# Attention values projected in the scan stage, key tiles turned one step later, layer 0's expert weights stored in the chip's tile layout

## The chip, the cores and the metric

The kernel runs on one core of a Trainium2 chip. The metric is the device time in microseconds of one execution of the whole program; lower is better. All arithmetic is in float32 except some masks in bfloat16.

## The reference

Two layers are applied to x (4 batches, 512 tokens, 512 features); `ctx` (4, 512, 256) is a second input.

```
x = x + mamba(ctx, layernorm(x))          # layer 0: selective scan, 512 channels x 16 states
x = x + moe0(layernorm(x))                # 32 experts, top 4, capacity 64, F = 352, and a shared expert
x = x + cross_attention(layernorm(x), ctx)  # layer 1: 16 heads of 32
x = x + moe1(layernorm(x))                # 32 experts in 8 groups, top 8, F = 256, and a shared expert
```

The cross attention, which the change touches most:

```
y_main, y_dca = ctx[:, :496], ctx[:, 496:]
q = ln(x @ Wq + bq)                     # per head, with weight and bias
k = ln(y_main @ Wk + bk);  v = y_main @ Wv + bv
out = softmax(q k^T * scale) v + softmax(q k_dca^T * scale) v_dca
out @ Wo + bo
```

The values `ctx @ Wv` depend on inputs only, not on anything that an earlier stage computes.

## The kernel before, in words

The program is a row of stages, each with one instruction stream per engine that is synchronised by semaphores; a stage ends with a barrier of all engines. The engines are TensorE (matrix products), VectorE, ScalarE and GpSimd; SyncE (SP) only issues DMAs.

**Scan stage** (`mamba_stage`, line 155). A loop of 64 iterations: 4 batches b, 16 states n each. In an iteration ScalarE makes `dA` (line 415), VectorE makes the input product and the scan (lines 505 and 511), GpSimd multiplies the states by C (line 285), and TensorE sums the products into `ps_y` (`total`, line 630). All are double buffered. Beside this, the same loop prepares batch b + 1: projection, convolution, the step sizes (`softplus` on TensorE at n = 12, its copies `summed` on ScalarE at n = 15), all through two PSUM banks `ps_w`. At n = 0 and 1 of the next batch TensorE turns the gated output of the last one back (`turned`). SP spreads rows of B and C over the partitions, four iterations ahead (`spread`). `ctxT`, the turned context of one batch, has one buffer.

**Layer 0's experts** (`expert_stage0`, line 1309). 16 tiles of 128 slots, two experts each. Weights of three tiles are held; SP loads those of tile t (`tile_weights`, line 1299) when the down projection of tile t - 3 is done. TensorE waits for all of a tile's loads before its gate product (line 1681). GpSimd adds each result to its tokens in DRAM by an indirect DMA (line 1437), one at a time: it waits for the landing of the one before. In DRAM the weights lie by expert as the reference has them, so a partition's row of a gate or up tile is 5632 contiguous bytes per expert, and one of a down tile 2048.

**Attention** (`attention_stage`, line 2051). The loop has 64 steps i: 4 batches b of n = 0 to 15, that is four groups g of four heads, four tiles j of 128 queries (for the scores that give the maxima) or keys (for the shifted scores). A step has, on TensorE, the shifted scores of i (line 2877), other work that the step number picks, and then the plain scores of i + 5 (line 2860), whose maxima VectorE takes (line 2616); ScalarE exponentiates the shifted scores (line 2378); GpSimd adds three of four probability tiles (lines 2241, 2248), and after four steps TensorE makes the sums (`SUM`, line 2893) and the weighted values (`PV`, line 2908; `DC` for the 16 DCA keys, line 2918). Step n = 0 has `PV` of the batch before.

The other work is named by a pair of letters: `K`, `Q`, `V` projections of the next batch's keys and queries and of this batch's values, `KT`, `QT` the normalised heads turned (line 2799), `XT` x turned, `M` the mixed queries, `AT` the turned maxima, `SD`, `PD` the DCA scores and probabilities, `WO` the output projection. All of these go through two PSUM banks, 6 and 7, in turn: the list `order` fixes the sequence, a name's bank is its number modulo 2, and `room(name)` makes TensorE wait until the name two places before it has been emptied by ScalarE or VectorE. The engines run their own instructions strictly in the order of the code. A head (K or Q tile) passes: TensorE projection, VectorE bias (`head_in`, line 2509), ScalarE square, VectorE variance (line 2519), GpSimd power and product (`head_norm`, lines 2224 and 2227), TensorE turn, ScalarE copy to `kT` or `rawq` (lines 2311, 2321). Heads have three buffers. In batch 0 the values and queries are made ahead of the loop. GpSimd also computes `rs`, the scale of the next batch's tokens (line 2218), which VectorE needs for `xn` (line 2499), and that is what `XT` turns.

In the steps 0 to 5 before the change, `order` reads for 1 <= b <= 2:

```
PV3 DC3 (b-1) SD0 K0 | SD1 K1 V0 V1 | M2 KT0 K2 V2 | V3 KT1 AT1 K3 XT0 PD0 SUM0 | PV0 DC0 KT2 Q0 | XT1 KT3 Q1
```

The exponentials of step i >= 4 wait until the `PV` that reads the same buffer is done, so those of n = 4 follow `PV0`.

## Time and profile before

| | us |
|---|---|
| median of 3 runs | 3114.5 (3114.5 to 3119.78) |
| profiled execution | 3106.26 |
| its span | 3104.5 |
| TensorE busy | 2687.9 (87%) |
| VectorE busy | 1493.2 (48%) |
| ScalarE busy | 773.7 (25%) |
| GpSimd busy | 1367.1 (44%) |

The span is the time from the first to the last record of one profiled execution. PE is TensorE, PEld its weight loads, DVE VectorE, ACT ScalarE, POOL GpSimd, SP the queue of SyncE. Busy shares are averages over stages with different limits; they say little on a change to one stage. L1681 is line 1681 of the kernel.

### The profile page before, as it was taken

The page shows a single profiled execution, that of the slowest core. Times are in us where ns is not written, and L with a number is a line of the kernel's source. Part 1 is how long each engine was busy: PE and PEld are TensorE (multiplying, and loading weights), DVE is VectorE, ACT ScalarE, POOL GpSimd, SP SyncE. Part 2 cuts the span into 40 slices and gives each one's busy share as a digit, 9 for nine tenths or more (in the row PEclk, how much of TensorE's full clock was granted, in tenths as well). Part 3 has the DMA queues.
Part 4 walks back from the last instruction along what each step waited for, and adds up shares of the span by engine and source line. Part 5 has one row for each costly group of instructions (what it writes and reads, how often), then busy time and mean ns, then how long its engine had stood idle before and what let it go on. Part 6 is the DMA issues. An engine that isn't in the chain of part 4 may idle for free. (4 is left out here: it accounts for less than half of the span.)

```text
span 3104.5 us, 33211 instructions
## 1 busy us (share of the span) xinstructions
PE 2687.9 (87%) x8933; PEld 1175.3 (38%) x8936; DVE 1493.2 (48%) x2766; ACT 773.7 (25%) x1190; POOL 1367.1 (44%) x960
## 2 busy tenths in 40 slices
PE   5888975799999887689999998981999999899995
PEld 2343431344444333233333334430444444444442
DVE  7999999332000232266666646310444444344442
ACT  4746653200000010133434332000121111111111
POOL 2777656143000131136646431465455555455555
PEclk8999999999999998889999999995999999999997
DMA  3334222310300599750474001555777776877664
GB/s 125 113 100 111 78 66 54 113 56 14 114 0 14 209 355 333 220 151 1 122 202 116 1 1 59 207 196 194 152 150 161 145 124 126 189 143 163 127 102 53
DMA packets 386408, 385.06 MB, mean 124 GB/s; under 512 B 72195, under 2 KB 311364, under 8 KB 386307
## 3 DMA queue, kind: packets, MB, share of 16 engines
q1 hardware_dynamic: 212434, 243.23, 25.0%
q0 software_dynamic: 68272, 97.19, 16.1%
q10 hardware_dynamic: 105600, 43.35, 6.6%
q8 instruction: 56, 0.92, 0.1%
q14 instruction: 46, 0.37, 0.0%
HBM read 236.15 MB, written 160.27 MB: 128 GB/s over the span
## 5 line engine op out<-in xcount | busy, mean ns | idle before, releaser
L1865 POOL DMA_INDIRECT out_x<-e_yo,e_dest x318 | 493.3, 1551 | 447.8 <-DMA out_x<-e_yo,e_dest 303.5
L2012 PE MATMUL e_psg<-e_wgu,e_xsT 128*128 x1272 | 578.3, 598 | 79.9 <-DVE e_xsT L1950 79.9
L285 POOL TENSOR_TENSOR hc<-hs,bcst 128x1024 f32<-128x1024 f32 x128 | 300.8, 2350 | 175.4 <-DVE ps_b L505 169.5
L2012 PEld LDWEIGHTS e_psg<-e_wgu,e_xsT 128*128 128x128 f32 x1272 | 233.1, 193 | 312.4 <-issue 312.4
L2028 PE MATMUL e_pso<-e_wd,e_hT 128*128 x636 | 306.2, 604 | 27.4 <-DVE e_hT L1955 26.7
L630 PE MATMUL ps_y<-hc,ident 128*128 128x512 f32 x512 | 242.5, 612 | 86.6 <-POOL hc L285 86.4
L511 DVE TENSOR_TENSOR_SCAN hs<-dA,ps_b 128x1024 f32<-128x1024 f32 x128 | 292.6, 2286 | 6.6 <-ACT dA L415 2.4
L1960 DVE TENSOR_TENSOR e_h<-e_psg,e_sg 128x256 f32<-128x256 f32 x159 | 67.3, 423 | 345.1 <-ACT e_sg L1886 335.3
L1233 PE MATMUL r_ps_t<-r_wd,r_h 128*128 128x512 f32 x480 | 209.6, 597 | 8.7 <-DVE r_h L982 5.1
L1886 ACT ACTIVATE e_sg<-e_psg 128x256 f32<-128x256 f32 x159 | 61.1, 384 | 543.9 <-PE e_psg L2012 538.5
L982 DVE TENSOR_TENSOR r_h<-r_ps_u,r_sg 128x512 f32<-128x512 f32 x60 | 41.4, 691 | 319.5 <-PE r_ps_u L1214 296.1
L415 ACT ACTIVATE dA<-dt,a_neg 128x511 f32<-128x511 f32 x256 | 165.4, 713 | 109.2 <-DVE hs L511 104.2
L2028 PEld LDWEIGHTS e_pso<-e_wd,e_hT 128*128 128x128 f32 x636 | 119.3, 191 | 188.5 <-issue 188.4
L2616 DVE TENSOR_REDUCE a_nm<-a_ps 128x2 f32<-128x992 f32 x128 | 146.1, 1185 | 88.9 <-PE a_ps L2860 88.5
L880 POOL DMA_INDIRECT slots_in<-r_xn,scat x128 | 126.6, 989 | 135.8 <-DMA slots_in<-r_xn,scat 60.3
L1893 ACT ACTIVATE e_yo<-e_pso,e_wrow 128x512 f32<-128x512 f32 x159 | 109.3, 687 | 288.4 <-PE e_pso L2028 217.4
L1950 DVE STREAM_TRANSPOSE e_xsT<-e_xs 128x512 f32<-128x512 f32 x159 | 174.6, 1098 | 12.8 <-DMA e_xs<-slots_in 7.3
L630 PEld LDWEIGHTS ps_y<-hc,ident 128*128 128x128 f32 x512 | 93.2, 192 | 230.7 <-POOL hc L285 135.7
L2378 ACT ACTIVATE a_pt<-a_ps 128x1024 f32<-128x1024 f32 (+1 forms) x128 | 126.2, 1022 | 184.0 <-PE a_ps L2877 123.3
L915 ACT ACTIVATE r_sg<-r_ps_g 128x512 f32<-128x512 f32 x60 | 35.8, 597 | 523.2 <-PE r_ps_g L1214 504.4
L505 DVE TENSOR_TENSOR ps_b<-du,bcst 128x1024 f32<-128x1024 f32 x128 | 159.3, 1244 | 8.3 <-DVE hs L511 0.5
L1214 PE MATMUL r_ps_g<-r_xnT,r_wgu 128*128 128x512 f32 x352 | 158.7, 593 | 0.0
(411 smaller groups left out, 3517.8 us busy)
## 6 DMA issues: line engine op xcount, KB each, us to landing
slots_in<-zeros SPq DMA_DIRECT2D x160, 256.0 KB, 2.3
e_xs<-slots_in ACTq DMA_DIRECT2D x160, 256.0 KB
bcst<-bc_rows SPq DMA_DIRECT2D x128, 256.0 KB, 4.3
e_wgu<-in_wg SPq DMA_DIRECT2D x32, 512.0 KB
e_wgu<-in_wu SPq DMA_DIRECT2D x32, 512.0 KB
e_wd<-in_wd SPq DMA_DIRECT2D x32, 512.0 KB
e_w<-in_wg SPq DMA_DIRECT2D x11, 1408.0 KB
e_w<-in_wu SPq DMA_DIRECT2D x11, 1408.0 KB
```

Of the source, the lines that this page charges most:

```text
L285: pool.tensor_tensor(hc[:, it % 2, half(h), :], hs[:, it % 2, half(h), :], bc(bcst[:, q, 1, :], 1, HB), ALU.mult).then_inc(sem["hc"], 1)
L415: i = act.activation(dA[:, it % 2, t, 1:], dt[:, b % 2, t, 1:], ACT.Exp, scale=a_neg[:, n, t:t + 1])
L505: dve.tensor_tensor(ps_b[:, :, :], du[:, b % 2, half(h), :], bc(bcst[:, q, 0, :], 1, HB), ALU.mult)\
L511: dve.tensor_tensor_scan(hs[:, it % 2, half(h), :].rearrange(flat), dA[:, it % 2, half(h), :].rearrange(flat), ps_b[:, :, :].rearrange(fla ...
L630: i = pe.matmul(ps_y[:, t, :], c["ident"][:, :], hc[:, it % 2, t, :], start=False, stop=False, skip_group_check=True)
L1214: i = pe.matmul(ps[:, f % 2, :], w[:, k, f * P:(f + 1) * P], xnT[:, b, k, :], start=k == 0, stop=k == KH - 1)
L1233: i = pe.matmul(ps_t[:, j % 2, :], h[:, f, j * P:(j + 1) * P], wd[:, f, :], start=f == 0, stop=f == FC - 1)
L1865: pool.indirect_dma_start(halves, bass.IndirectOffsetOnAxis(dest[:, q, a:a + 1], 0), yo[:, q, a * HC:(a + 1) * HC], None, bounds_check=2 * ...
L1950: dve.transpose(xsT[:, q % 2, :, :].rearrange("p k (s j) -> p k s j", j=DQ), xs[:, q // RING % 2, part, :].rearrange("p s (i k) -> p k s i ...
L2012: j = pe.matmul(ps_g[:, q % 2, :], xsT[:, q % 2, k, :], wgu[:, bass.ds(e % RING, 1), k, :], start=k == 0, stop=k == KH - 1)
L2028: j = pe.matmul(ps_o[:, q % 2, :], hT[:, q % 2, a, :], wd[:, bass.ds(e % RING, 1), a, :], start=a == 0, stop=a == NW - 1)
L2616: dve.tensor_reduce(nm[:, i % 8, 2 * z:2 * z + 2], ps[:, at:at + 2, 0:S2], AX_X, ALU.max, negate=True)\
```

## The change

1. *Scan stage.* It gets the weights `w_v` (loaded before the first row spreads), a buffer `vals`, and `values(b, ts)` on TensorE, ScalarE and SP: 16 projections of context tiles by `w_v`, copied and stored to a DRAM tensor `values`. Those of batches 1 to 3 are made at n = 13 and 14 of the batch before on TensorE and copied at n = 15 and n = 1 on ScalarE; those of batch 0 in the last batch, whose context is read again. The context loads move from n = 10 to n = 0, and `turned` waits for all four copies in the place of the step sizes.
2. *Attention.* The value projections, their copies and the weights `wv` go; SP reads the values of a batch from DRAM once `PV3` of the batch before has been computed. The zero fills that SP issues in batch 0 wait for nothing. `K3` moves ahead of the scores in n = 3; `KT1`, `KT2`, `KT3` move from n = 3, 4, 5 to n = 4, 5, 6; VectorE takes K3's bias at the start of n = 3 instead of after its maxima.
3. *Layer 0's weights.* The host stores, for a pair of experts, each partition's gate, up and most of the down weights in one row (`pair0`), and the last 96 rows of the down weights in `rest0`. `tile_weights` has three loads instead of six (four of them for down), and the down product reads its last chunk from its own view.

```diff
-    for w in ("wg", "wu"):
-        load(W[w].rearrange("p e k f -> p e (k f)"), I[w + "0"][2 * t:2 * t + 2, :, :].rearrange("e (p k) f -> p e (k f)", k=KH))
-    for z in range(2):
-        load(W["wd"][:, z, 0:2, :], I["wd0"][2 * t + z, 0:2 * P, :].rearrange("(c p) n -> p c n", p=P))
-        load(W["wd"][0:FR, z, 2, :], I["wd0"][2 * t + z, 2 * P:F0, :])
+    g = 4 * KH * F0
+    load(W["gate_up"], I["pair0"][t, :, 0:g])
+    load(W["down"], I["pair0"][t, :, g:])
+    load(W["down_rest"][0:FR, :], I["rest0"][t, :, :])
...
-        order += now(("SD", 1)) + new(("K", 1)) + late(("V", 0), ("V", 1))
-        order += now(("M", 2)) + new(("KT", 0), ("K", 2)) + late(("V", 2))
-        order += late(("V", 3)) + new(("KT", 1)) + now(("AT", 1)) + new(("K", 3), ("XT", 0)) + now(("PD", 0), ("SUM", 0))
-        order += now(("PV", 0), ("DC", 0)) + new(("KT", 2), ("Q", 0))
-        order += new(("XT", 1), ("KT", 3), ("Q", 1))
-        order += now(("M", 3)) + new(("XT", 2), ("Q", 2), ("QT", 0))
+        order += now(("SD", 1)) + new(("K", 1))
+        order += now(("M", 2)) + new(("KT", 0), ("K", 2))
+        order += new(("K", 3)) + now(("AT", 1)) + new(("XT", 0)) + now(("PD", 0), ("SUM", 0))
+        order += new(("KT", 1)) + now(("PV", 0), ("DC", 0)) + new(("Q", 0))
+        order += new(("XT", 1), ("KT", 2), ("Q", 1))
+        order += now(("M", 3)) + new(("XT", 2), ("KT", 3), ("Q", 2), ("QT", 0))
...
# SP, scan stage
+                sp.dma_start(w_v[:, :, :], I["wkv"][:, H:].rearrange("(k p) n -> p k n", p=P)).then_inc(sem["wvin"], 16)
                 for it in range(RING):
                     spread(it)
...
# ScalarE, scan stage
+                        if n == 1:
+                            values(b, (2, 3))
...
                         if n == 15:
                             summed(b + 1, range(TB))
+                            values(b + 1, (0, 1))
...
# TensorE, scan stage
+                def values(b, ts):
+                    turn = turn_of_values(b)
+                    pe.wait_ge(sem["wvin"], 16)
+                    pe.wait_ge(sem["ctxin"], 16 * (turn + 2))
+                    for t in ts:
+                        if t >= 2:
+                            pe.wait_ge(sem["vcopied"], TB * turn + t - 1)
+                        elif b > 0:
+                            pe.wait_ge(sem["dt"], TB * (b + 1))
+                        else:
+                            pe.wait_ge(sem["xadd"], TB * (B - 1))
+                        for k in range(KC):
+                            i = pe.matmul(ps_w[:, t % 2, :], ctxT[:, k, t * P:(t + 1) * P], w_v[:, k, :],
+                                          start=k == 0, stop=k == KC - 1)
+                        i.then_inc(sem["vmm"], 1)
...
# SP, attention
+                    if b == 0:
+                        context(2)
+                    else:
+                        landed(sp, ("PV", b - 1, NG - 1))
+                        values_in(b)
...
# ScalarE, attention
                     if more:
                         if n == 4:
                             squared(("K", b + 1, 3))
-                            keys(b + 1, 2)
+                            keys(b + 1, 1)
```

## Rows read from the trace of the kernel before

**Rows 1.** Stages: stretch, us; busy by engine; TensorE's clock, DMA share, GB/s.

```profile
0.00:552.00 552.00, 429.51 (x992) 178.57 (x993) 513.27 (x391) 296.20 (x440) 338.05 (x192) 0.95 0.32 91
...
1057.00:1283.00 226.00, 171.73 (x864) 77.58 (x864) 63.36 (x190) 24.44 (x42) 50.22 (x48) 0.89 0.94 305
...
1283.00:1882.00 599.00, 540.77 (x3168) 217.37 (x3168) 352.29 (x422) 213.90 (x274) 287.55 (x192) 0.96 0.35 95
```

**Rows 2.** Timeline (start, us, what, [idle before]) of SP and VectorE, scan start.

```profile
32.77 38.66 SPq L229 DMA_DIRECT2D bcst<-bc_rows  x12
...
48.44 1.23 DVE L505 TENSOR_TENSOR ps_b<-du,bcst 128x1024 f32<-128x1024 f32 x1
```

**Rows 3.** Timeline of TensorE, ScalarE, VectorE at the first batch boundary of the scan.

```profile
160.28 8.75 PE L630 MATMUL ps_y<-hc,ident 128*128 128x512 f32 x20
...
160.98 4.99 ACT L415 ACTIVATE dA<-dt,a_neg 128x511 f32<-128x511 f32 x8
...
168.29 2.29 DVE L511 TENSOR_TENSOR_SCAN hs<-dA,ps_b 128x1024 f32<-128x1024 f32 x1
```

**Rows 4.** Stretches, TensorE's timeline and the scatters' landing: layer 0's experts (third: attention).

```profile
1190.00:1194.00 4.00, 4.00 (x29) 2.10 (x26) 0.00 (x0) 0.46 (x1) 0.09 (x1) 1.00 1.02 391
...
1197.50:1200.00 2.50, 1.23 (x6) 0.14 (x2) 0.00 (x0) 0.69 (x1) 0.00 (x0) 1.00 1.08 264
...
1290.00:1297.00 7.00, 5.95 (x14) 3.46 (x15) 1.93 (x7) 1.20 (x2) 2.32 (x2) 0.56 1.05 393
...
1188.99 2.59 PE L1681 MATMUL e_psg<-r_wgu,e_xsT 128*64 128x352 f32 x16 [1.94 <-issue]
...
1203.35 4.57 PE L1681 MATMUL e_psg<-e_w,e_xsT 128*64 128x352 f32 x16 [4.62 <-issue]
...
x_after<-e_yo,e_dest POOLq DMA_INDIRECT x16, 8.6
```

**Rows 5.** Attention's costliest groups, and TensorE's timeline ahead of its loop.

```profile
L2767 PE MATMUL a_ps<-a_wv,a_ctxT 128*128 128x512 f32 x64 | 31.0, 608 | 7.7 <-DVE a_hd L2509 7.3 <-ACT a_v L2338 0.3
...
1302.94 1.96 PE L2767 MATMUL a_ps<-a_wv,a_ctxT 128*128 128x512 f32 x4 [0.87 <-DVE a_hd L2509]
...
1304.73 0.60 PE L2799 MATMUL a_ps<-ident,a_hd 128*128 128x128 f32 x4
...
1324.08 1.95 PE L2823 MATMUL a_ps<-a_rawq,a_mix 128*128 128x512 f32 x4 [0.96 <-ACT a_rawq L2321]
```

**Rows 6.** Timeline of GpSimd and TensorE in batch 1, n = 1 to 3.

```profile
1486.44 2.91 POOL L2224 TENSOR_TENSOR a_hr<-a_hv,minus_half 128x16 f32<-128x16 f32 x1 [18.34 <-DVE a_hv L2522]
...
1505.38 1.02 POOL L2218 TENSOR_TENSOR a_rs<-a_ve,minus_half 128x4 f32<-128x4 f32 x1
...
1509.02 0.60 PE L2786 MATMUL a_ps<-ident,a_xn 128*128 128x128 f32 x4
...
1510.34 1.09 PE L2843 MATMUL a_ps<-ident,a_sd 128*64 128x128 f32 x8 [0.72 <-DVE a_hd L2509]
...
1511.36 1.06 PE L2893 MATMUL a_ps<-a_acc,a_one 128*32 128x512 f32 x8
```

**Rows 7.** Timeline of TensorE and ScalarE in batch 1, n = 4.

```profile
1517.86 1.12 PE L2918 MATMUL a_ps<-a_pdT,r_xnT 64*128 64x512 f32 x2
...
1517.99 1.94 ACT L2378 ACTIVATE a_pt<-a_ps 128x1024 f32<-128x1024 f32 x2 [4.05 <-PE a_ps L2908]
...
1520.80 0.69 ACT L2311 ACTIVATE r_xnT<-a_ps,a_one 128x512 f32<-128x512 f32 x1 [0.35 <-PE a_ps L2799]
```

**Rows 8.** Waits of TensorE in batch 0 and the clock behind the second.

```profile
1367.94 1.08 PE L2799 MATMUL a_ps<-ident,a_hd 128*128 128x128 f32 x4 [4.29 <-POOL a_hd L2227]
...
1434.13 1.08 PE L2799 MATMUL a_ps<-ident,a_hd 128*128 128x128 f32 x4 [3.30 <-POOL a_hd L2227]
...
1434.00:1441.00 7.00, 6.87 (x26) 2.52 (x26) 0.51 (x1) 3.30 (x4) 6.51 (x6) 0.61 0.00 0
```

**Rows 9.** Timeline of TensorE in batch 3, the start of the sums.

```profile
1779.62 1.07 PE L2893 MATMUL a_ps<-a_acc,a_one 128*32 128x512 f32 x8
```

More of the change, by code:

```diff
@@ L2413, in _ @@
                             squared(("K", b + 1, 2))
-                        if b > 0:
-                            value(b, 3)
-                        if more:
-                            keys(b + 1, 1)
                             turned_x(b + 1, 0)
@@ L2961, in _ @@
                     if n == 3:
-                        if late:
-                            value(b, 3)
                         if more:
-                            turn_head("K", b + 1, 1)
+                            key(b + 1, 3)
                         turn_max(b, 1)
+                    if n == 4 and more:
+                        turn_head("K", b + 1, 1)
                     if n in (4, 8, 12):
```

139 lines of the change are left out of this document (81 added, 58 removed).

## The prediction

> **What bounds the kernel now.** I read the stages first (busy time by stretch), then who waits inside each. The scan stage has VectorE busy 513 of 552 us; layer 0's experts (1057 to 1283 us) have the DMA engines at 0.94 of all their time, while TensorE has 172 of 226 us; attention has TensorE busy 541 of 599 us [rows 1]; layer 0's route and everything behind attention are not touched. So the change adds work to a stage that VectorE bounds, alters transfers in a stage that DMA bounds, and takes matmuls from a stage that looks bound by TensorE. The profiled execution took 3106.26 us (span 3104.5), 8.2 us under the median of the runs, 3114.5. I sum against the former and carry the difference to the median.
>
> **Part 1, values made in the scan stage: +2.5 us.** 16 projections (4 instructions each), 16 ScalarE copies and 16 stores of 256 KB are added, 0.5 MB of weights and the context blocks that are read again.
> *At the start* the w_v load stands ahead of the first row spreads on SP's queue. They are issued from 32.77 us, and VectorE first needs one at 48.44 [rows 2]. 0.5 MB at 391 GB/s [rows 4] is 1.3 us: hidden in those 15. The value stores stand before spreads that run three to four iterations (7 us each) ahead: hidden too.
> *At the three batch boundaries* I walk the new chain. TensorE ends the softplus sums and begins the running sums at 160.28; these take 8.75/20 us an instruction, so `total(12)` (8 instructions) ends at 163.8 and two values (8 more) at 167.3; the copy behind them (0.7 us, as the key copy of [rows 7]) ends at 168.0, and only then ScalarE, in order, starts dA(15), which it started at 160.98. Two of these at 4.99/8 us give 169.2; VectorE's scan wants them at 168.29 [rows 3]: 0.9 us late, three times. The other two values wait for the copies and are followed by sums with slack; those of the last batch (n = 6 to 9) have over 4 us before their dA. Bounds: 0 (the copy is right on time) to 5 us (1.7 at each boundary, if each of the four values is one instruction slower than I take it). I take 2.5, the walk's.
>
> **Part 2, layer 0's weights as on chip: -14 us.** Each of 16 tiles needs 2.88 MB of gate and up (512 rows of 5632 B before) and 1.44 MB of down weights (704 rows of 2 KB), by six DMAs; after, three DMAs of 128 rows of 22.5 KB, 128 of 8 KB and 96 of 4 KB. The bytes are the same. TensorE waits before each gate product (1.94, 4.62 us) and tiles follow at 1203.35 - 1188.99 = 14.4 us [rows 4], the pace of the transfers; its own work is about 11 us, so any gain down to that comes through. The stretch with gate and up rows runs at 391 GB/s, that with only down rows at 264, both with the engines full [rows 4]. If the down weights moved at 391, they would take 3.7 instead of 5.5 us: 1.8 us a tile is the upper bound. The lower bound is 0: 2 KB rows can run fast (at 1290 to 1297 us the loads of x, 2 KB rows too, run at 393 GB/s [rows 4]), so length alone isn't proven to be what slows the down rows. I take 1.1 us, nearer to the first, since fewer, longer rows also spare turnarounds. It counts for the 13 tiles after the queue is full (3 to 15): -14, between -23 and 0. The stage's tail (last tile, last scatter) is unchanged.
> The Trainium skill, in "DMA: Bandwidth & Descriptors", section "Where 436 GB/s comes from", says that for transfers from HBM the memory side binds at about 358 GB/s a core. The 391 and 393 GB/s of rows 4 speak against it. By that rule a tile's 4.9 MB could not take less than 13.6 us, and part 2 would be at most -10.
>
> **Part 3, attention: +3 us, not the -39 that it removes.** The value projections are 31.0 us of TensorE with 7.7 us of waits before them [rows 5]. What is late next, piece by piece:
> *Before the loop.* Each round goes query, value, turned head; the turned head (1304.73) waits for the value's 1.8 us (from 1302.94), and the next head's square on ScalarE stands behind the copy of the turned head, so the round's whole loop over four engines is 1.8 longer. Three rounds count (in the fourth the value lies beside the norm that ends late): -5.4, the first mix at 1318.7 instead of 1324.08 [rows 5]; bounds 0 and -7.2.
> *n = 0 to 3, batches 0 to 2.* Only the order on TensorE changes, but GpSimd, in order, does the norms of K0 and K1, both additions and the token scale without a gap: 1486.44 to 1506.40 [rows 6]; that start hangs on K0 and the DCA scores, which stay. The token norm (0.54) and `XT0` need the scale. So XT0 can start at 1507.1 instead of 1509.02, and as K3's bank is by then long empty (it cost 0.72), the sums start at 1508.65 instead of 1511.36 [rows 6]: -2.7, not the 11 us of values and waits that stood there. TensorE now waits about 4.9 us before XT0. Batch 0: the wait of 4.29 us for K1's norm [rows 8] goes and comes back in the same way: -2.1.
> *n = 4.* The new order puts KT1, PV0, DC0. DC0 takes the bank of KT1, and ScalarE empties KT1 only after exp(i4), which waits for PV0, and after the square of K3. That chain stands in the trace [rows 7]: PV0 ends at 1517.9, the exponentials start at 1517.99, the key copy behind them starts at 1520.80 and takes 0.7; in the new order there is no wait for a turn within it, so it ends 3.2 us after PV0. DC0 started directly after PV0 (1517.86) and now starts 3.2 us later: +3.2, and +0.05 of KT2 that moved behind. n = 6: KT3 wants M3's bank, which ScalarE empties 3.7 us after the step's start, where TensorE is after 2.6; half is regained, since the queries waited there before: +0.65. In all +3.9 for each of three batches.
> *Batch 3* has no keys, only values: 7.2 us of TensorE (four of 1.8). Without them the maxima of i = 7, which VectorE starts after the DCA probabilities, hold TensorE for about half of that; the sums start near 1776.1 instead of 1779.62 [rows 9]: -3.5; bounds 0 and -7.2.
> Sum: -5.4 + (3.9 - 2.1) + 2(3.9 - 2.7) - 3.5 = -4.7.
> *The clock.* After 3.30 us without work (1430.8 to 1434.1) TensorE ran a 7 us stretch at 0.61 of its 2.4 GHz, so mostly at 1.2 [rows 8]: 7 x 0.39 = 2.7 us lost. The new waits of 4.9 and 3.2 us come in three batches, six in all; batch 0 has one such loss already. I price the first of each pair at 2.7 less that one (5.4) and the second at half of the chance (4): +8 or so, between 0 and +14. Attention: +3.3, between -5 and +9, and -38 if my chain is wrong.
> *The rest of part 3:* value reads (1 MB, asked for at n = 0, needed at n = 4, 25 us later) are hidden; the zero fills start some 20 us earlier beside GpSimd's adding reads of x, which are needed only in n = 2 of batch 0; context 0 and the value weights no longer load, as many bytes of values do instead: 0.
>
> **Sum:** 2.5 - 14 + 3.3 = -8, so 3098 for a profiled execution like this one and 3106.5 for the median.
>
> **Rivals.**
> *A, removed matmuls come through:* the GpSimd chain has slack that I don't see, or the bank wait is covered. For it: TensorE 541 of 599 us busy. Against: [rows 6, 7], which are program order. Attention -25 to -38, total about 3073. Chance 0.10.
> *B, the weights are no faster:* the 264 GB/s comes from where the rows land, not from their length. For it: 2 KB rows at 393. Against: fewer rows and DMAs. Total 0 + 2.5 + 3.3 = +6: 3120; by halves 3113. The skill's rule above belongs here: it would give 3110. Chance 0.20.
> *C, slower: the scatter-adds wait behind long rows.* They share the engines with the weights; each needs the one before it. Landing takes 8.6 us now [rows 4], with 8 rows of 2 KB on each engine. If each of the 8 has to wait for a row of 22.5 KB (0.92 us at 391/16 GB/s) instead of 5.6 KB (0.23), landing is 14.1, and with the 1.5 us that GpSimd's instruction takes the cycle is 15.7 us against 14.4, +1.3 x 13 = +17, total 3137. It eats into part 2 once landing passes 11.7 us and makes the whole slower above about 12.9. Against: many of the weights' rows are shorter, and three output buffers smooth it. The same page, section "Queues, rings and completion order", has an engine change queues only between packets of several descriptors; by it the wait would be as long or longer. Chance 0.10.
> *D, slower by the clock:* all six waits cost a low stretch as long as rows 8 and part 2 brings little: +9 + 2.5 - 5 = +6.5, 3121. Chance 0.12.
> Forecast: 0.48, within 3099 to 3113.
>
> About 0.2% (6.2 us) is what a measurement tells from no change. Faster by more: 0.35 of the forecast's 0.48, A, and a little of B: 0.48. Slower by more: C, half of D, some of B: 0.20. Between: 0.32. Eight times in ten: 3090 to 3122.
>
> **What would show it.** In the experts of layer 0: tiles 13.3 us apart, waits before the gate product remain, no 264 GB/s stretch (right); 14.4 (B); 15 and scatter landings over 12 us (C). In attention: TensorE's wait before XT0 ends with the token norm, released by GpSimd's scale; a wait of 3 us before DC0 released by ScalarE's key copy in batches 0 to 2; TensorE busy about 30 us less with as little gain. In the scan: VectorE waits about 0.9 us for dA at three places. It is wrong if the attention stage is over 10 us shorter than 599, or the experts' stage is not 5 us shorter than 226.

## The result, and the profile after

The changed kernel takes 3126.2 us in the median of 20 runs (3114.0 to 3134.4), the one before 3114.5 in as many. The ratio is 1.0041, with a 95% interval of 1.0029 to 1.0053: 13 us slower, 9 to 16. The prediction was 3106.5, within 3090 to 3122: it forecast a gain, and the time lies above its range.

The profiled execution has a span of 3126.8 us. By stage, in us, each measured from its first mark to the next one's in the trace:

| kernel | scan | layer 0's experts | attention | layer 1's experts | span |
|---|---|---|---|---|---|
| before | 554.2 | 229.9 | 583.9 | 939.8 | 3104.5 |
| changed | 559.2 | 225.8 | 599.0 | 949.1 | 3126.8 |

(The marks: start of the span, first statistics behind the scan; GpSimd's iota of the expert stage, its first `rs` of attention, the first statistics behind attention; the second iota of layer 1's experts, their last scatter. The two route stages differ by 2 us or less.) Layer 1's experts are not touched. In the profiles below they take 935.6 to 949.1 us whatever was edited, so their +9 is the difference of one execution from another. The verdicts come from the medians.

The stages as windows of the changed kernel, beside [rows 1]. The columns are, here and below: length, busy time of TensorE, of its weight loads, of VectorE, ScalarE and GpSimd, then TensorE's granted clock (1.00 is 2.4 GHz), the DMA engines' busy share, and GB/s.

```profile
0.00:557.00 557.00, 453.15 (x1056) 191.73 (x1057) 514.53 (x391) 304.08 (x456) 338.24 (x192) 0.96 0.35 100
...
1061.00:1286.00 225.00, 169.03 (x864) 77.09 (x864) 66.43 (x193) 24.44 (x42) 49.31 (x48) 0.89 0.94 313
1286.00:1897.50 611.50, 534.02 (x3104) 213.94 (x3104) 352.57 (x419) 205.56 (x258) 288.67 (x192) 0.93 0.35 96
```

TensorE's busy time in attention fell by 7 us, from 541 to 534, though 31 us of value projections are gone: its clock went from 0.96 to 0.93, and what is left ran slower.

**Scan.** TensorE, ScalarE and VectorE at the first batch boundary, beside [rows 3] (a timeline: start, us, what, and in brackets the idle time before it and what ended that):

```profile
160.49 3.60 PE L685 MATMUL ps_y<-hc,ident 128*128 128x512 f32 x8
163.92 3.60 PE L646 MATMUL ps_w<-w_v,ctxT 128*128 128x512 f32 x8
167.36 3.60 PE L685 MATMUL ps_y<-hc,ident 128*128 128x512 f32 x8
```

```profile
165.84 0.60 ACT L398 ACTIVATE vals<-ps_w 128x512 f32<-128x512 f32 x1 [4.55 <-PE ps_w L646]
167.56 0.60 ACT L398 ACTIVATE vals<-ps_w 128x512 f32<-128x512 f32 x1 [1.12 <-PE ps_w L646]
168.05 4.99 ACT L456 ACTIVATE dA<-dt,a_neg 128x511 f32<-128x511 f32 x8
```

```profile
169.46 2.29 DVE L552 TENSOR_TENSOR_SCAN hs<-dA,ps_b 128x1024 f32<-128x1024 f32 x1 [1.00 <-DVE ps_b L546]
```

The copies of the first two values end at 168.2, dA(15) starts only then (168.05), and the scan waits 1.0 us for it; 1.01 and 1.02 at the other two boundaries.

**Layer 0's experts.** Two stretches, TensorE's gate products and the scatters' landing, beside [rows 4]:

```profile
1176.00:1178.00 2.00, 1.86 (x8) 0.94 (x10) 0.80 (x1) 0.00 (x0) 0.00 (x0) 0.50 0.99 391
...
1200.00:1202.00 2.00, 2.00 (x12) 0.48 (x8) 1.35 (x9) 0.00 (x0) 1.38 (x1) 1.00 1.18 258
```

```profile
1190.90 4.18 PE L1747 MATMUL e_psg<-r_wgu,e_xsT 128*64 128x352 f32 x16 [2.89 <-issue]
...
1205.33 4.96 PE L1747 MATMUL e_psg<-e_w,e_xsT 128*64 128x352 f32 x16 [3.11 <-issue]
```

```profile
x_after<-e_yo,e_dest POOLq DMA_INDIRECT x16, 13.0
```

The slow stretch, 258 GB/s with the engines full, is still there, though no weight row is shorter than 4 KB now; these tiles are 14.4 us apart as before. The scatters land after 13.0 us instead of 8.6.

**Attention, ahead of the loop,** beside [rows 5]: TensorE, VectorE, GpSimd.

```profile
1315.19 1.08 PE L2851 MATMUL a_ps<-ident,a_hd 128*128 128x128 f32 x4 [3.60 <-DVE a_hd L2587]
1319.94 1.09 PE L2851 MATMUL a_ps<-ident,a_hd 128*128 128x128 f32 x4 [3.67 <-DVE a_hd L2587]
1321.99 3.75 PE L2875 MATMUL a_ps<-a_rawq,a_mix 128*128 128x512 f32 x4 [0.96 <-ACT a_rawq L2394]
1325.67 2.71 PE L2912 MATMUL a_ps<-r_xnT,a_qT 32*128 32x496 f32 x12
```

```profile
1305.35 0.17 DVE L2579 TENSOR_SCALAR a_hv<-a_hv 128x16 f32<-128x16 f32 x1
...
1310.23 3.55 DVE L2579 TENSOR_SCALAR a_hv<-a_hv 128x16 f32<-128x16 f32 x1
```

```profile
1309.25 4.49 POOL L2307 TENSOR_TENSOR x_resid<-x_resid,a_bo 128x2048 f32<-128x2048 f32 x1 [7.59 <-DMA a_bo<-in_bo]
```

**Attention, batch 1, n = 3 and 4,** beside [rows 6, 7]: GpSimd's scale, TensorE, and ScalarE's copy of KT1.

```profile
1509.81 1.01 POOL L2291 TENSOR_TENSOR a_rs<-a_ve,minus_half 128x4 f32<-128x4 f32 x1
```

```profile
1511.55 1.06 PE L2838 MATMUL a_ps<-ident,a_xn 128*128 128x128 f32 x4 [5.04 <-DVE a_xn L2556]
1512.54 1.97 PE L2895 MATMUL a_ps<-ident,a_sd 128*64 128x128 f32 x8
1514.44 1.32 PE L2945 MATMUL a_ps<-a_acc,a_one 128*32 128x512 f32 x8
...
1518.21 3.64 PE L2959 MATMUL a_ps<-a_pt,a_v 128*32 128x512 f32 x32
1525.00 1.87 PE L2969 MATMUL a_ps<-a_pdT,r_xnT 64*128 64x512 f32 x2 [3.15 <-ACT r_xnT L2384]
1526.80 2.03 PE L2912 MATMUL a_ps<-a_kT,a_qT 32*128 32x496 f32 x8
```

```profile
1524.26 0.69 ACT L2384 ACTIVATE r_xnT<-a_ps,a_one 128x512 f32<-128x512 f32 x1
```

TensorE waits 5.04 us before XT0 (before the change it had value and key projections to do there), and what follows runs at half speed: XT0 1.06 us (0.60 before), the probabilities 1.97 (1.09). It waits 3.15 us before DC0, for ScalarE's key copy, and again DC0 takes 1.87 (1.12) and the scores 2.03 (1.26).

### The profile page after: what moved, and what is told of

It reads as the page before. It is cut to its first block and busy times, and to the rows that moved or that the text cites. A ratio compares the mean times of both kernels' runs of the same rounds, so it can differ in the third digit from the quotient of the medians.

```text
span 3126.8 us, 33176 instructions
## 1 busy us (share of the span) xinstructions
PE 2698.1 (86%) x8935; PEld 1181.8 (38%) x8936; DVE 1497.7 (48%) x2766; ACT 773.3 (25%) x1190; POOL 1367.8 (44%) x960
## 5 line engine op out<-in xcount | busy, mean ns | idle before, releaser
L2017 DVE STREAM_TRANSPOSE e_xsT<-e_xs 128x512 f32<-128x512 f32 x159 | 174.4, 1097 | 12.4 <-DMA e_xs<-slots_in 6.9
```

Source lines behind the costliest of these rows:

```text
L2017: dve.transpose(xsT[:, q % 2, :, :].rearrange("p k (s j) -> p k s j", j=DQ), xs[:, q // RING % 2, part, :].rearrange("p s (i k) -> p k s i ...
```

## Experiments

All ratios are to the kernel before, with the 95% interval. "The changed kernel" stands at 1.0041.

**1. The parts alone.** `only_weights` and `only_scan` are the kernel before with one part; `no_weights` is the changed kernel with the six old loads.

```diff
 # no_weights, against the changed kernel (only_weights has these lines the other way round)
-    load(W["gate_up"], I["pair0"][t, :, 0:g])
-    load(W["down"], I["pair0"][t, :, g:])
-    load(W["down_rest"][0:FR, :], I["rest0"][t, :, :])
+    for w in ("wg", "wu"):
+        load(W[w].rearrange("p e k f -> p e (k f)"), I[w + "0"][2 * t:2 * t + 2, :, :].rearrange("e (p k) f -> p e (k f)", k=KH))
+    for z in range(2):
+        load(W["wd"][:, z, 0:2, :], I["wd0"][2 * t + z, 0:2 * P, :].rearrange("(c p) n -> p c n", p=P))
+        load(W["wd"][0:FR, z, 2, :], I["wd0"][2 * t + z, 2 * P:F0, :])
 # only_scan, against the kernel before: ScalarE in the scan stage (TensorE and SP as in the change)
                             summed(b + 1, range(TB))
+                            values(b + 1, (0, 1))
```

> The kernel before with nothing but layer 0's weights in the new layout (three loads a tile instead of six). Theory 1, from the two traces: the stage from its first gate product to its last took 202.6 us before and 198.9 after, so this kernel is 3 to 5 us faster than the one before (ratio 0.9985) and its tiles follow each other at 14.3 us as before. Theory 2, the prediction's term: the down rows were slow for their 2 KB, 14 us faster (0.9955), tiles at 13.3 us. Theory 3, the prediction's rival B: no gain at all, 1.000.

> The kernel before with the values made and stored in the scan stage as in the changed kernel, while attention still projects its own: the price of part 1 alone. Theory 1, from the two traces: +4.8 us (three late dA of 1.0 us at the batch boundaries, 0.6 at the second one more for du, and 1.3 at iterations 25 and 26 of one batch), ratio 1.0015, first statistics behind the scan at 559 instead of 554. Theory 2, the prediction's term: +2.5 us, 1.0008.

> The changed kernel with layer 0's weights loaded as before: parts 1 and 3. Theory 1: +4.8 and the attention stage's +15, so 18 to 20 us slower than before, ratio 1.006, and the difference to the kernel with part 1 alone is attention's own price, 13 to 16 us. Theory 2, the prediction's terms: +2.5 + 3.3 = 6 us, 1.002. Theory 3: the attention stage of the one profile was an unlucky one, and the difference to part 1 alone is under 6 us.

| kernel | median us | ratio | scan | layer 0's experts | attention |
|---|---|---|---|---|---|
| only_weights | 3106.1 | 0.9984 (0.9972 to 0.9995) | 554.8 | 224.6 | 583.2 |
| only_scan | 3112.3 | 1.0011 (0.9999 to 1.0023) | 561.0 | 230.0 | 581.1 |
| no_weights | 3131.0 | 1.0073 (1.0057 to 1.0089) | 558.9 | 228.4 | 592.9 |

Part 1 costs 3.4 us (0 to 7). The other two parts can each be had in two ways. The weights are worth 5 us (2 to 9) on the kernel before, and 10 (4 to 16) by the changed kernel against no_weights. Attention costs 19 us (13 to 25) by no_weights against only_scan, and 14 (8 to 21) if only_weights and only_scan are taken off the changed kernel. The intervals allow one value for both ways, and either way the three parts add up to the +13. In profiles the attention stage takes 592.9 to 599.0 us in five executions with the changed attention (changed, no_weights, copies_behind, short_rows, rest_first) and 581.1 to 583.9 in three with the old: 9 to 18 us.

only_weights and no_weights fit theory 1 and exclude the prediction's sizes (0.9955 and 1.002). only_scan does not tell them apart: 1.0015 and 1.0008 both lie in its interval.

**2. Is it the wait or the clock?** TensorE is given products to do in its two new waits. They go to a bank of the scores that is free and is overwritten next.

```diff
+                def filler(which, i, n):
+                    vacant(which, i, 0)
+                    for _ in range(n):
+                        pe.matmul(ps[:, pair_bank(which, i, 0), :], ident[:, :], wq[:, 0, :], start=True, stop=True)
...
                     if n == 3 and more:
+                        filler(2, i + 1, 5)        # 11 in "filled"
                         turn_x(b + 1, 0)
...
                         weigh(b, n // TB - 1)
+                        if n == 4 and more:
+                            filler(1, i + LEAD, 3) # 7 in "filled"
                         weigh_d(b, n // TB - 1)
```

> The changed kernel with TensorE kept at work in its two new waits of batches 0 to 2: 11 products of 128x512 into a free bank of the scores ahead of the turned x of n = 3 (wait 5.0 us), 7 between PV0 and DC0 (wait 3.15 us); their results are overwritten. The waits themselves stay as long. Theory 1, the clock: the granted clock falls after each wait and costs 2.0 us (x, probabilities and sums at half speed) and 3.2 us (DC0, scores, a query) in each of three batches; kept busy, the clock stays at 1.0 there and the kernel is 12 to 16 us faster than the changed kernel, back at about the time of the one before (1.000 to 1.001 of it). Theory 2, the waits alone are the price and the clock is priced as in the prediction (8 us in all, 2.7 of it in batch 0 before too): 3 to 6 us faster than the changed kernel. Theory 3: fillers only lengthen the chain: slower than the changed kernel.

3129.8 us, 1.0073 (1.0055 to 1.0091): 10 us slower than the changed kernel. By the letter that is theory 3, but I had sized the fillers wrong: one float32 product stands as two instructions in the profile (11 products are x22), so they outlasted the waits by 4.5 and 3.1 us. Behind them the clock was full (XT0 0.60 us, DC0 1.12). So once more at the right length:

> The changed kernel with fillers of the right length. In the run named filled each product of 128x512 was two instructions in the profile, so 22 and 14 of them lasted 9.7 and 6.3 us in waits of 5.0 and 3.15 us; the clock stayed at 1.0 behind them, but the chain was 4.5 and 3.1 us longer. Now 5 and 3 products (4.4 and 2.6 us), so the waits end when they did. Theory 1, the clock: 4 to 5 us less in each of three batches, 12 to 15 us faster than the changed kernel, ratio to the kernel before 0.999 to 1.001; XT0, the probabilities and DC0 take 0.60, 1.09 and 1.12 us instead of 1.06, 1.97 and 1.87. Theory 2, what the low stretches cost is mostly covered by other waits that then grow: 0 to 6 us faster than the changed kernel.

3106.4 us, 0.9987 (0.9975 to 1.0): 17 us faster than the changed kernel, by adding 24 dummy products. TensorE of filled_short in batch 1, fillers included:

```profile
1498.73 4.56 PE L2936 MATMUL a_ps<-r_xnT,ident 128*128 128x512 f32 x10
1503.85 0.63 PE L2838 MATMUL a_ps<-ident,a_xn 128*128 128x128 f32 x4 [0.56 <-DVE a_xn L2556]
1504.40 1.09 PE L2895 MATMUL a_ps<-ident,a_sd 128*64 128x128 f32 x8
...
1512.52 2.84 PE L2936 MATMUL a_ps<-r_xnT,ident 128*128 128x512 f32 x6
1515.74 1.12 PE L2974 MATMUL a_ps<-a_pdT,r_xnT 64*128 64x512 f32 x2 [0.38 <-ACT r_xnT L2384]
1516.79 1.11 PE L2912 MATMUL a_ps<-a_kT,a_qT 32*128 32x496 f32 x8
```

XT0, the probabilities, DC0 and the scores are back at 0.63, 1.09, 1.12 and 1.11 us. The data arrive no sooner; only the clock differs. Without the low stretches the changed kernel is 17 us faster (12 to 22), which is all that attention costs in experiment 1. Not all of the 17 need be new, though: in its profile the kernel before also has a low stretch in these steps of batch 0 (the first half of the sums, at 1378.13, takes 1.94 us, and 1.06 in the batches behind it).

**3. The wait before DC0.**

```diff
-        order += new(("KT", 1)) + now(("PV", 0), ("DC", 0)) + new(("Q", 0))
+        order += now(("PV", 0), ("DC", 0)) + new(("KT", 1), ("Q", 0))
```

(and `turn_head("K", b + 1, 1)` behind `weigh_d` on TensorE)

> The changed kernel with KT1 behind DC0 instead of ahead of PV0 in n = 4, so that DC0 no longer takes the bank that ScalarE empties last. Theory 1: the wait of 3.15 us before DC0 and the low clock behind it (3.2 us) go in batches 0 to 2, 6.4 us a batch, 17 to 19 us faster than the changed kernel, ratio to the kernel before 0.998 to 0.9995. Theory 2: the wait only moves (to the query behind KT1, or to XT1): under 8 us faster than the changed kernel.

3105.4 us, 0.9976 (0.9963 to 0.9989): 20 us (15 to 26) faster than the changed kernel, theory 1, and with this one move also 7 us (3 to 12) faster than the kernel before. TensorE of key_behind: PV0 and DC0 follow each other again, at full speed.

```profile
1509.57 3.64 PE L2959 MATMUL a_ps<-a_pt,a_v 128*32 128x512 f32 x32
1513.14 1.12 PE L2969 MATMUL a_ps<-a_pdT,r_xnT 64*128 64x512 f32 x2
```

**4. The wait before XT0.**

```diff
                         if n == 2:
                             head_norm(("K", b + 1, 1))
-                        if n == 3:
                             token_scale(b + 1)
+                        if n == 3:
                             head_norm(("K", b + 1, 2))
```

> The changed kernel with GpSimd's scale of the next batch's tokens ahead of its second addition (n = 2) instead of behind it. The scale's input is ready 1.2 us before GpSimd ends K1's norm. Theory 1, GpSimd's chain holds XT0: the scale is done at 1505.9 instead of 1510.8 in the profile's time, VectorE's token norm at about 1508.5 instead of 1511.4, the wait of 5.0 us before XT0 falls to 2; then the sums wait for the second addition, which now ends 1 us later (1510.9): 3 us less a batch, 9 us in all, and up to 15 if TensorE's clock no longer falls there. Theory 2, VectorE's order holds XT0 (its K3 bias, K2 variance and the shift of the queries stand ahead of the token norm): under 3 us in all.

3113.9 us, 1.0009 (0.9997 to 1.002): 10 us (5 to 15) faster than the changed kernel, theory 1. TensorE of scale_ahead in batch 1, and then in batch 0:

```profile
1510.90 0.63 PE L2838 MATMUL a_ps<-ident,a_xn 128*128 128x128 f32 x4 [2.28 <-DVE a_xn L2556]
1511.46 1.09 PE L2895 MATMUL a_ps<-ident,a_sd 128*64 128x128 f32 x8
1513.20 1.06 PE L2945 MATMUL a_ps<-a_acc,a_one 128*32 128x512 f32 x8 [0.65 <-issue]
```

```profile
1377.34 1.09 PE L2838 MATMUL a_ps<-ident,a_xn 128*128 128x128 f32 x4 [2.29 <-DVE a_xn L2556]
1378.35 1.97 PE L2895 MATMUL a_ps<-ident,a_sd 128*64 128x128 f32 x8
```

The wait is 2.28 us instead of 5.04. In batches 1 and 2 the clock does not fall behind it (0.63, 1.09); in batch 0 it does, behind a wait as long (1.09, 1.97). The sums now start 0.65 us late, while GpSimd's second addition ends.

**5. The long VectorE instruction.**

```diff
-                biased(0)
                 for i in range(NU):
                     b, n, G = i // NQ, i % NQ, i // TB
+                    if i == 0:
+                        pool.wait_ge(sem["exp"], 1)
+                        biased(0)
```

> The changed kernel with GpSimd's addition of the output bias to batch 0's rows (4.5 us) behind the first exponentials instead of inside the preparation of the first queries. In the profile a VectorE instruction on 128x16 numbers that takes 0.17 us elsewhere took 3.55 us while that addition ran, and TensorE waited 3.6 us for it. Theory 1, the two engines get in each other's way: that instruction takes 0.17 us again, the loop starts 3.4 us earlier, and the kernel is 3 to 6 us faster than the changed one (ratio to the kernel before 1.002 to 1.003). Theory 2, the long instruction is a wait of another cause: no change (1.004).

3118.5 us, 1.0025 (1.0014 to 1.0037): 5 us (0 to 10) faster, theory 1. VectorE of bias_later, the same instruction, and TensorE's last two turned heads and first mixes:

```profile
1309.14 0.17 DVE L2581 TENSOR_SCALAR a_hv<-a_hv 128x16 f32<-128x16 f32 x1
```

```profile
1310.72 0.63 PE L2853 MATMUL a_ps<-ident,a_hd 128*128 128x128 f32 x4 [0.22 <-DVE a_hd L2589]
1315.02 0.63 PE L2853 MATMUL a_ps<-ident,a_hd 128*128 128x128 f32 x4 [3.67 <-DVE a_hd L2589]
1316.60 3.75 PE L2877 MATMUL a_ps<-a_rawq,a_mix 128*128 128x512 f32 x4 [0.96 <-ACT a_rawq L2396]
```

Of the two waits the addition made only the first, 3.60 us, now 0.22. The second, 3.67, stays, and so do the mixes at half speed.

**6. The walk in the scan stage.**

```diff
                         if n == 15:
                             summed(b + 1, range(TB))
-                            values(b + 1, (0, 1))
                     ...                       # the dA of this iteration
+                    if b < B - 1 and n == 15:
+                        values(b + 1, (0, 1))
```

> The changed kernel with ScalarE's copies of the first two values behind dA of n = 15 alone: the step of the prediction that walked from TensorE's products to that dA. Theory 1, the walk holds: VectorE's waits of 1.0 us at three batch boundaries go, 3 us faster than the changed kernel (ratio to the kernel before 1.003), first statistics behind the scan near 556 instead of 559. Theory 2, the cost of part 1 is only the added work on the queues: no change (1.004, 559).

3117.3 us, 1.003 (1.0016 to 1.0043): 3 us faster by the medians, which the intervals do not tell from no change. The profile does show theory 1: the first statistics behind the scan come at 553.7, no later than before, and VectorE no longer waits at the three boundaries. At the first one:

```profile
166.72 1.22 DVE L547 TENSOR_TENSOR ps_b<-du,bcst 128x1024 f32<-128x1024 f32 x1
167.97 2.29 DVE L553 TENSOR_TENSOR_SCAN hs<-dA,ps_b 128x1024 f32<-128x1024 f32 x1
```

**7. Which rows make layer 0's experts slow?** First row length and the scatters:

```diff
 # short_rows
-    load(W["gate_up"], I["pair0"][t, :, 0:g])
+    for r in range(4):
+        load(W["gate_up"][:, r * KH * F0:(r + 1) * KH * F0], I["pair0"][t, :, r * KH * F0:(r + 1) * KH * F0])
 # no_scatter
-                    pool.indirect_dma_start(D["x0"][:, :], ...)
+                    pool.dma_start(D["x0"][t:t + 1, 0:H], yo[0:1, t % RING, :]).then_inc(sem["out"], 16)
```

> The changed kernel with layer 0's gate and up weights fetched by four DMAs a tile with rows of 5632 B instead of one with rows of 22528 B (the bytes, and where they lie in DRAM, are the same). Theory 1, a row of 5.6 KB is already long enough, since the bytes per ns of an engine are the same in both traces: the same time as the changed kernel within 2 us, tiles 14.3 us apart. Theory 2, long rows hold up the scatters behind them (the prediction's rival C): the scatters land sooner and the kernel is 2 to 6 us faster. Theory 3, long rows are what gave the gain: 3 to 5 us slower.

> The changed kernel without the addition of layer 0's expert results to the tokens (one small DMA a tile stands in its place), so what follows routes other numbers and only the stage of layer 0's experts is read. Theory 1, the engines' time is the sum of all rows moved: without the scatter's 512 rows in four tiles the tiles follow at about 12.9 us instead of 14.3, and the stretches under 300 GB/s between the weights go. Theory 2, the weights alone set the pace (a limit of the memory): tiles at 14.3 us as before, at a lower busy share of the DMA engines.

short_rows: 3122.5 us, 1.0052 (1.0032 to 1.0072), no different from the changed kernel. The scatters do land sooner (9.5 us instead of 13.0), and the stage is not shorter (230.1): theory 1, against rival C. no_scatter: tiles 13.6 us apart, between the two theories, and the slow stretch stays (219 GB/s from 1190 to 1192 us). Then the other two kinds of rows:

```diff
 # no_slot_rows, from tile 4 on
-                    sp.dma_start(xs[:, t % XR, :], D["xs0"][t * P:(t + 1) * P, :])
+                    sp.dma_start(xs[:, t % XR, H:], D["xs0"][t * P:(t + 1) * P, H:])
 # no_rest
-    load(W["down_rest"][0:FR, :], I["rest0"][t, :, :])
+    load(W["down_rest"][0:FR if t < 3 else 1, :], I["rest0"][t, 0:FR if t < 3 else 1, :])
```

> The changed kernel with the slots' rows of layer 0's experts from tile 4 on fetched without their 512 features (128 rows of 128 B instead of 2176 B, 256 KB less a tile; the products take the features of an earlier tile), so only this stage is read. Theory 1: these rows are what slows the stretch between the down weights and the next gate weights; without them the stretches of 208 to 264 GB/s go and the tiles follow at 13.0 us or less instead of 14.3 (256 KB at 391 GB/s alone would be 0.7 us). Theory 2: they cost what their bytes cost: 13.6 us, and the slow stretch stays.

> The changed kernel with the last down weights (96 rows of 4 KB, 384 KB a tile) fetched in one row only from tile 3 on, so the down products take old weights; only the stage of layer 0's experts is read. Theory 1: the 4 KB rows onto 96 of 128 partitions are what slows that stretch: tiles at 12.7 us or less and no stretch under 300 GB/s. Theory 2: they cost what their bytes cost (384 KB at 391 GB/s is 1.0 us): tiles at 13.3, and the slow stretch stays.

And whether it is their 96 partitions or their place:

```diff
 # rest_wide, from tile 3 on: the same bytes onto 128 partitions
+        load(W["down_rest"][:, 0:2 * H * FR // P], I["rest0"][t, :, :].rearrange("p n -> (p n)").rearrange("(q m) -> q m", q=P))
 # rest_first: the load of down_rest ahead of the other two
```

> The changed kernel with the same 384 KB of last down weights from tile 3 on fetched as 128 rows of 3 KB onto all 128 partitions instead of 96 rows of 4 KB onto 96 (the down products then find other numbers there, so only the stage of layer 0's experts is read). In the run named no_rest the tiles were no longer held up by the weights at all, and 9% fewer bytes gave about 2.4 us a tile, where their bytes alone would cost 1.0. Theory 1, the 96 partitions are the cause: tiles at 13.0 us or less, over 360 GB/s from 1133 to 1233 us. Theory 2, it is the transfer as such (a third one, at the end of each tile's): 14.3 us and 340 GB/s as in the changed kernel.

> The changed kernel with those last down weights (96 rows of 4 KB) asked for ahead of the tile's other two transfers instead of behind them. Theory 1, the 96 partitions are the cause: no change, tiles at 14.3 us, ratio to the kernel before 1.003 to 1.005. Theory 2, it is the end of a tile's transfers that is slow, where the next tile's slot rows and weights come in: 2 to 10 us faster, since then 8 KB rows stand at the end.

no_scatter, no_slot_rows, no_rest and rest_wide leave data out or put it in other places, so only this stage is read, and each was run once. The same 100 us of each kernel (the last two columns are the DMA engines' busy share and GB/s). The kernel before:

```profile
1133.00:1233.00 100.00, 75.64 (x372) 34.00 (x370) 25.84 (x79) 8.62 (x15) 14.90 (x10) 0.88 1.04 341
```

The changed kernel:

```profile
1133.00:1233.00 100.00, 73.06 (x369) 33.55 (x369) 26.75 (x79) 8.62 (x15) 14.16 (x9) 0.91 1.03 339
```

no_scatter:

```profile
1133.00:1233.00 100.00, 80.99 (x418) 36.53 (x414) 28.62 (x87) 10.98 (x19) 7.91 (x10) 0.91 1.02 355
```

no_slot_rows:

```profile
1133.00:1233.00 100.00, 80.31 (x395) 38.37 (x397) 26.69 (x79) 9.60 (x17) 14.72 (x9) 0.90 1.03 340
```

no_rest:

```profile
1133.00:1233.00 100.00, 88.25 (x505) 40.63 (x501) 31.68 (x100) 12.08 (x21) 17.93 (x11) 1.00 0.97 367
```

rest_wide:

```profile
1133.00:1233.00 100.00, 84.86 (x453) 39.36 (x451) 31.44 (x97) 10.23 (x18) 14.24 (x11) 0.95 1.02 399
```

rest_first:

```profile
1133.00:1233.00 100.00, 75.17 (x356) 33.91 (x356) 27.16 (x80) 9.71 (x17) 14.90 (x9) 0.86 1.03 332
```

| kernel | tiles apart once weights are waited for, us | first to last gate product, us |
|---|---|---|
| before | 14.4 | 202.6 |
| changed | 14.3 | 198.9 |
| no_scatter | 13.6 | 186.0 |
| no_slot_rows | 13.6 | 190.8 |
| no_rest | 9.5 to 11.2 | 165.0 |
| rest_wide | 12.1 | 174.8 |
| rest_first | 14.9 | 207.9 |

Scatters and slot rows cost about what their bytes cost. The 96 rows cost far more: without them TensorE hardly waits for weights, and with the same 384 KB spread over 128 partitions all rows together move at 399 GB/s instead of 339, and the stage is 24 us shorter. Put first, they are as dear: rest_first took 3125.2 us, 1.0061 (1.0044 to 1.0077), and its tiles are 14.9 us apart. So it is the transfer onto 96 partitions, not its place, the slots, the scatters or the gate rows' length; rest_wide's rows are also shorter (3 KB for 4), but mended_wide below keeps 4 KB. The kernel before had the same 96 partitions, in two loads of 192 KB a tile.

The records of single rows in these 100 us show where the time goes. A 4 KB row takes 255 ns in the mean on 96 partitions and 159 ns on 128 (mended_wide; a 3 KB row of rest_wide 121). And the rows of the other transfers are slower beside the 96: 151 ns instead of 88 for 2176 B, 359 instead of 318 for 8 KB, 938 instead of 843 for 22.5 KB (changed kernel, rest_wide). If the rows are dealt out evenly (6 of the 96 an engine, 8 of every 128), that is 2.2 us a tile between these two kernels, the whole of 14.3 less 12.1. No run separates the number of partitions from how the rows are dealt out to the 16 engines.

**8. Versions that beat both.** `mended` is the changed kernel with the edits of 3, 4, 5 and 6. `mended_warm` also fills TensorE's waits ahead of the loop (14 products before the first turned x, 4 and 1 later). `mended_wide` is mended with `rest0` stored as 128 rows:

```diff
-    load(W["down_rest"][0:FR, :], I["rest0"][t, :, :])
+    load(W["down_rest"], I["rest0"][t, :, :])
...
-    i["rest0"] = f(wd0[:, :, 2 * P:, :].transpose(0, 2, 1, 3).reshape(E // 2, F0 - 2 * P, 2 * H))
+    i["rest0"] = f(np.pad(wd0[:, :, 2 * P:, :].transpose(0, 2, 1, 3).reshape(E // 2, F0 - 2 * P, 2 * H),
+                          ((0, 0), (0, 3 * P - F0), (0, 0))))
```

> The changed kernel with four moves and nothing taken out: KT1 behind DC0, GpSimd's token scale ahead of its second addition, the addition of the output bias behind the first exponentials, and in the scan stage ScalarE's copies of the first two values behind dA of n = 15 instead of ahead of it. Theory 1, the costs are separate and add: 20 + 10 + 5 us as the three alone gave, and 3 of the scan stage: 3088 to 3092 us, ratio to the kernel before 0.993 to 0.994. Theory 2, they overlap (each clears up the same low stretches of TensorE's clock): 3096 to 3102, 0.996 to 0.9975.

3084.5 us, 0.9932 (0.9913 to 0.9952): theory 1, 21 us (15 to 27) faster than the kernel before. Its profile has attention at 564.3 us and the scan at 553.3.

> The kernel named mended with TensorE kept at work ahead of attention's loop: 14 products of 128x512 while it waits 20 us for the first token norm, 4 and 1 in the waits of 3.67 and 0.96 us before the last turned head and the first mix (all into a bank of the scores that is free then). Theory 1, the clock: the queries (8.7 us), mixes (3.75), first scores (2.76 + 8.66) and maxima (1.94) ran largely at half speed, and of these the chain keeps 3 to 6 us: ratio to the kernel before 0.991 to 0.992. Theory 2: these waits belong to VectorE's and ScalarE's chain of norms and maxima, which the clock doesn't touch: under 2 us (0.993).

3087.9 us, 0.9937 (0.9918 to 0.9955): no gain, theory 2. The mixes ran at full speed (1.96 us instead of 3.75), but the scores behind them took 8.66 us as in mended. My reading is that they wait for VectorE's maxima; that was not tested. Behind them the clock fell after all.

> The kernel named mended with the last down weights stored as 128 rows of 4 KB (the 32 rows behind the 96 are zeros and never read), so that this transfer goes to all 128 partitions and takes 512 KB instead of 384. In rest_wide, with 384 KB on 128 partitions, tiles followed at 12.1 us and the stage from its first to its last gate product took 174.8 us instead of 198.9. Theory 1, partitions count: 128 KB more at 400 GB/s are 0.3 us a tile, 12.4 us, the stage is 20 us shorter, and the whole takes 3064 to 3070 us, ratio to the kernel before 0.987. Theory 2, the gain of rest_wide was its 3 KB rows: tiles at 14.6 us or more, 0.993 to 0.995.

3065.2 us, 0.9878 (0.9857 to 0.9899): theory 1, 17 us (8 to 26) faster than mended and 38 us (31 to 44) faster than the kernel before. Stretch and gate products of mended_wide (tiles 12.4 us apart):

```profile
1133.00:1233.00 100.00, 81.14 (x427) 37.57 (x428) 30.58 (x93) 9.76 (x17) 12.40 (x8) 0.95 1.02 402
```

```profile
1186.70 4.14 PE L1748 MATMUL e_psg<-e_w,e_xsT 128*64 128x352 f32 x16 [2.69 <-issue]
...
1199.09 2.59 PE L1748 MATMUL e_psg<-e_w,e_xsT 128*64 128x352 f32 x16 [1.10 <-issue]
```

## Why the prediction was wrong, step by step

| term | predicted, us | measured, us |
|---|---|---|
| part 1, scan | +2.5 (0 to 5) | +3.4 in runs, +5.0 in the profile |
| part 2, weights | -14 (-23 to 0) | -5 or -10 in runs, -4 in the profile |
| part 3, attention | +3.3 (-5 to +9) | +14 or +19 in runs, +15 in the profile |
| sum | -8 | +13 |

(Two numbers are the two ways of experiment 1: -10 goes with +19, -5 with +14. Of the 21 us between the forecast and the measured change, part 3 makes 11 to 16, part 2 the rest but 1.)

*Part 1 was right in its mechanism.* The walk gave 0.9 us late at three boundaries; it was 1.0, and in the profile of copies_behind the waits are gone. The 2 us more in the profile are knock-ons that the walk didn't follow: at iterations 25 and 26 a VectorE product took 1.93 us instead of 1.26 and the wait for a dA grew from 0.50 to 1.10; at 31 the four `du` took 3.55 us instead of 2.95.

*Part 2 failed in the term "if the down weights moved at 391".* I read the stretch at 264 GB/s as that of the 2 KB rows [rows 4] and took the length for the cause, of which I had noted myself that 2 KB rows also run at 393. Lengthening the rows left the stretch in place, and from the seventh tile to the fifteenth the pace is 14.3 us in both kernels. The other reason that I gave for 1.1 us a tile, that fewer and longer rows spare turnarounds, no run shows either: short_rows, with six loads a tile and no row over 8 KB, is no slower. What was slow is that the last 96 rows of each expert's down weights go onto 96 of 128 partitions, which the change kept. The Trainium skill, "SBUF — State Buffer", section "Door 1: The DMA port swizzle (why [64,N] ≈ [32,N])", says that a transfer's rate depends on how many of 16 ports its partitions reach, and that partitions 0 to 63 reach only the 8 even ones. By that page's table of ports 96 partitions load the even ports twice as much as the odd ones, so as an estimate 384 KB should cost what 512 KB do on all 128. rest_wide and mended_wide agree in direction, but the 96 cost more than that: tiles are 14.3 us apart with them and 12.4 with 512 KB on 128. The 358 GB/s of the Trainium skill that the prediction weighed is passed for 100 us on end (399 and 402 GB/s), and the measurement decides.

*Part 3 had the chain right and the clock wrong.* The starts of the weighted values PV cut the stage into stretches. "Old" is the range over the kernel before, only_scan and only_weights, "new" over the five executions with the changed attention; us:

| from, to | predicted change without the clock | old | new | filled_short |
|---|---|---|---|---|
| stage's start, first PV0 | -7.5 | 92.0 to 94.9 | 90.7 to 96.4 | 89.7 |
| PV0, PV1 (batches 0 to 2) | +3.9 | 38.3 | 43.2 to 44.9 | 41.6 |
| PV3, next PV0 (batches 1, 2) | -2.7 | 43.1 | 42.2 to 43.6 | 40.8 to 40.9 |
| PV3, PV0 of batch 3 | -3.5 | 29.7 | 26.7 to 28.2 | 27.0 |

In filled_short, with the clock kept up in the six waits, the loop does nearly what the chain said: +3.3, -2.3, -2.7. So the waits were right. GpSimd's chain from K0 to the scale (18.9 us before, 18.8 after) sets XT0, which came 2.1 us sooner against SD0 (I had put it 1.9 sooner); the wait before it is 5.0 us (4.9); the wait before DC0 is 3.15 (3.2), released by ScalarE's key copy. Failed:
- *"The clock, +8 or so, between 0 and +14."* I gave the second wait of each pair half the chance of a low stretch, and took one stretch off the first. Both waits cost in every batch: from XT0 to PV0 1.5 us, from DC0 to the end of the first query 3.3 (changed kernel against filled_short), or 14 us for three batches by rows, 17 by the medians. This is rival D's mechanism, which had 0.12, at nearly its price. (The two parts that I named, 5.4 and 4, also make 9.4, not 8; that changes nothing here.)
- *"Before the loop, -5.4."* In the changed kernel the first mix came only 1.2 us sooner after the stage's start. The shorter rounds moved one of VectorE's instructions on 128x16 numbers under GpSimd's addition of the bias, where it took 3.55 us instead of 0.17 and ended with the addition (1313.8 and 1313.7); before, that addition fell between such instructions. TensorE waited 3.60 us for it. With the addition moved, in bias_later, the first mix comes 30.6 us after the stage's start, against 36.3 before: -5.7, the predicted step. The Trainium skill, "SBUF — State Buffer", section "Who interferes with whom", has VectorE and GpSimd share a port pair that is locked for a whole instruction; bias_later agrees (0.17 us, and 5 us of the whole).

*The rivals.* A is excluded: nothing of the 31 us came through. B's mechanism came: what counts is where the rows land, as rest_wide and mended_wide show. Its size, no gain at all, did not (only_weights: 5 us, 2 to 9). D was right in the clock. C's landing time came (13.0 us; I had 14.1 for the worst case), but the tiles did not wait for it: short_rows has it at 9.5 with no gain.

*Left open:* why the 96 partitions cost more than their share of the ports; why the same kernel loses more to the clock in one execution than in another (PV0 to PV1 is 43.2 in one and 44.9 in another, the start to the first PV0 differs by 6 us), which spreads the profiles of attention over 9 to 18 us; and the 14 us by which the untouched last stage differs between executions.

By the prediction's own tests: the experts' stage was to be 5 us shorter than 226 and was 4 shorter; the 264 GB/s stretch was to go and stayed. TensorE was to be busy about 30 us less in attention and was 7 less (534 against 541), since what was left ran slower.

## What to carry to other kernels

Before taking work off the engine that looks like the bound, list what it will wait for instead, and put beside each new wait on TensorE the stretch at half clock behind it (here a wait of 3.15 us lost another 3.3 behind it); matmuls that only filled a wait were earning their time. A DMA rate that is low with the engines full is to be tied to one kind of row by leaving that row out, not by its length, and a tile that ends at partition 96 is worth padding to 128. An instruction that got twenty times longer in place tells of an engine beside it.

## What the runs showed of the hardware that I had not expected

- A transfer of 384 KB a tile onto 96 partitions holds the whole core's DMA at 339 GB/s; onto 128 partitions it is 399, and 402 with 128 KB of zeros more. A 4 KB row took 255 ns on the 96 and 159 on the 128, and rows of other transfers beside the 96 slowed too (88 to 151 ns for 2176 B).
- Adding 24 dummy products of 128x512 made a program 17 us faster (1.0041 to 0.9987), since the granted clock stayed at 2.4 GHz. In the changed kernel it fell after the waits of 3.15 and 5.04 us in every batch; in scale_ahead, after 2.28 us in the place of the 5.04, it did not fall in batches 1 and 2, and did in batch 0 (2.29 us), so the length of the wait alone does not decide.
- VectorE took 3.55 us (4.47 in no_weights) for 128x16 numbers while GpSimd added 128x2048 (4.49 us), and 0.17 otherwise.
- With weight rows of 22.5 KB beside them the scatters landed after 13.0 us instead of 8.6, and with gate rows of 5.6 KB again after 9.5, without a gain in the pace of the tiles.
